# A two-sequence selective scan: the last 128 columns of the second sequence are given to GpSimd, and nobody scales u ahead any more

## The reference

```python
def step(h, inp):
    dt, bt, ct, xt = inp
    h = jnp.exp(dt[:, :, None] * A) * h + (dt * xt)[:, :, None] * bt[:, None, :]
    y = jnp.einsum('bdn,bn->bd', h, ct)
    return (h, y)
...
x = _layernorm(x + out_proj(y + x * D_param))
x = _layernorm(x + down(silu(gate(x)) * up(x)))
```

## Time and profile before

| | |
|---|---|
| median of 3 runs | 2693.13 us (2690.42 to 2694.03) |
| time of the profiled execution | 2687.74 us |
| its span, from first to last instruction | 2685.9 us |
| mean granted TensorE clock | 0.956 of full speed |
| instructions | 48350 |

### The profile page before, as it was taken

The page is one execution under the profiler, slowest core; times in us unless marked ns, Lnnn a source line. Parts: engine busy times, 40 slices in busy tenths (PEclk is TensorE's granted clock), DMA queues, the critical chain, the costliest instruction groups (busy, mean ns, idle before and its releaser), DMA issues.

```text
span 2685.9 us, 48350 instructions
## 1 busy us (share of the span) xinstructions
PE 2316.6 (86%) x17036; PEld 1290.5 (48%) x17036; DVE 2584.4 (96%) x4160; ACT 1708.6 (64%) x2229; POOL 1028.3 (38%) x1031
## 2 busy tenths in 40 slices
PE   7866678998789987899779997799977998899998
PEld 4322224554345543555345553455534554465567
DVE  6999999999999999999999999999999999999892
ACT  5687766667566665667656666566666667654643
POOL 2343333443434434344333443344333443344320
PEclk8999999999999989999889998899989999999899
DMA  4566665777667876678757786577866777788694
GB/s 171 197 213 227 228 236 211 281 277 270 237 223 277 284 266 223 238 275 292 254 195 247 279 290 243 201 267 277 278 241 209 279 279 271 239 289 308 228 357 151
DMA packets 192060, 672.16 MB, mean 250 GB/s; under 512 B 20944, under 2 KB 26064, under 8 KB 191824
## 3 DMA queue, kind: packets, MB, share of 16 engines
q1 hardware_dynamic: 152432, 544.02, 57.5%
q10 hardware_dynamic: 39392, 125.06, 13.3%
HBM read 660.61 MB, written 8.39 MB: 249 GB/s over the span
## 4 chain that ended last, share of the span: by engine, by line
PE 39%; DVE 28%; ACT 15%; issue 12%; DMA 6%; POOL 0%; ACTq 0%; DVEq 0%; POOLq 0%
DVE h L709 14%; PE banks L1200 11%; DVE banks L686 10%; PE banks L1036 10%; PE banks L1176 7%; PE banks L1276 7%; ACT a L981 6%; DVE h L706 4%; DMA u_bc<-u_scratch 4%; ACT L720 2%; DMA U<-in_xT 1%; PE banks L1128 1%; PE banks L1124 1%; ACT u_bc L1000 1%; ACT v L862 1%
## 5 line engine op out<-in xcount | busy, mean ns | idle before, releaser
L981 ACT ACTIVATE a<-banks 128x2048 f32<-128x2048 f32 x512 | 960.7, 1876 | 604.3 <-PE banks L1200 563.1
L686 DVE TENSOR_TENSOR banks<-a,h 128x512 f32<-128x512 f32 x2048 | 1324.1, 688 | 4.1 <-ACT a L981 4.1
L709 DVE SCALAR_TENSOR_TENSOR h<-u_bc,BCt,banks 128x512 f32<-128x512 f32 x1482 | 1038.2, 732 | 5.4 <-PE banks L1276 5.4
L581 POOL TENSOR_TENSOR dexp<-spread,dt 128x512 f32<-128x512 f32 x512 | 539.1, 1053 | 821.2 <-DVE banks L686 779.2
L1200 PE MATMUL banks<-dexp,A 32*128 32x256 f32 x8192 | 623.6, 421 | 150.6 <-ACT a L981 149.0
L1276 PE MATMUL banks<-h,cz 128*32 128x512 f32 x4096 | 667.9, 623 | 94.4 <-DVE h L706 64.7
L1200 PEld LDWEIGHTS banks<-dexp,A 32*128 32x128 f32 x8192 | 390.3, 195 | 484.4 <-ACT a L981 347.7
L1036 PE MATMUL banks<-vT,w_ring 128*128 128x256 f32 x1792 | 449.9, 394 | 7.6 <-ACT up L948 6.9
L1036 PEld LDWEIGHTS banks<-vT,w_ring 128*128 128x128 f32 x1792 | 323.8, 190 | 175.4 <-issue 118.2
L706 DVE TENSOR_TENSOR h<-u_bc,banks 128x512 f32<-128x512 f32 x566 | 367.5, 673 | 19.9 <-PE banks L1276 19.9
L593 POOL TENSOR_SCALAR u_bc<-u_bc,BCt 128x512 f32<-128x512 f32 x266 | 184.1, 692 | 404.6 <-DVE banks L686 394.3
(11 more groups left out here) (177 smaller groups left out, 1284.9 us busy)
## 6 DMA issues: line engine op xcount, KB each, us to landing
u_bc<-u_scratch SPq DMA_DIRECT2D x1021, 512.0 KB, 4.6
w_ring<-in_gu_w ACTq DMA_DIRECT2D x112, 512.0 KB, 5.5
w_ring<-in_down_w ACTq DMA_DIRECT2D x56, 512.0 KB, 5.7
a<-in_gu_w ACTq DMA_DIRECT2D x16, 512.0 KB, 12.7
a<-in_down_w ACTq DMA_DIRECT2D x8, 512.0 KB, 4.4
x_tok<-in_x_rows SPq DMA_DIRECT2D x15, 256.0 KB, 5.7
out_rows<-v ACTq DMA_DIRECT2D x15, 256.0 KB, 3.4
U<-in_xT ACTq DMA_DIRECT2D x7, 512.0 KB, 6.0
```

Source lines behind the costliest of these rows:

```text
L581: e.tensor_tensor(dexp[:, q % E_RING, :, :, :], spread[:, :].unsqueeze(1).unsqueeze(1).to_broadcast(shape), by_step[:, :, first:first + BS ...
L686: e.tensor_tensor(m_ps[:, b, :], a[:, blk % A_RING, b, s, :], h[:, (t - 1) % H_RING, b * D:(b + 1) * D], ALU.mult).then_inc(s_m, 1)
L709: e.scalar_tensor_tensor(h[:, t % H_RING, part], u_bc[:, t % U_RING, part], BCt[c % 2][:, 0, b * TB + tl:b * TB + tl + 1], m_ps[:, b, :], ...
L981: e.activation(dst.rearrange("p b t (x j) -> p x (b t) j", j=GP), src.rearrange("p g (i r j) -> p (g i) r j", i=PAIR, j=GP), ACT.Exp, scal ...
```

## The change

VectorE keeps the first sequence and columns 0 to 383 of the second, so its second product and its second sum are 384 columns wide. The last 128 columns (`SHARE`) are made by GpSimd alone, with three instructions a step in the new `share`: the product of `a` and h(t-1) into `m_share` in SBUF, u by B in place, and their sum into h(t). The sum waits for both by semaphore, and the next step's product for the sum (`s_hg`). All scaling of u ahead, by GpSimd and by ScalarE, goes, and with it line 706; VectorE always uses the scaling form. GpSimd no longer waits on `s_m` ahead of its diagonals and pieces. What reads h or frees u, `a` or B now also waits for GpSimd's semaphores. A matrix of one value becomes a broadcast column, which makes room for `m_share`.

```diff
-        even = range(FIRST_Z, SEQ - 4, 2)
-        on_pool = {(t + 2, 0): i for i, t in enumerate(
-            t for t in even if not any(stage in PIECES for stage, _ in at_steps(t, 2)))}
-        on_act = {place: i for i, place in enumerate(
-            place for t in even if quiet(t) and light(t) and light(t - 2) for place in ((t + 2, 1), (t + 3, 0), (t + 3, 1)))}
...
                 if t >= U_RING:
                     e.wait_ge(s_h, BATCH * (t - U_RING + 1))
+                    e.wait_ge(s_hg, t - U_RING + 1)
...
-            def scale(t):
...
+            def share(t):
+                c, blk, s, tl, slot = t // TB, t // BS, t % BS, t % TB, t % U_RING
+                part, of_b = slice(BATCH * D - SHARE, BATCH * D), slice(D - SHARE, D)
+                if s == 0:
+                    e.wait_ge(s_exp, 2 * (blk + 1))
+                if t:
+                    e.wait_ge(s_hg, t)
+                e.tensor_tensor(m_share[:, :], a[:, blk % A_RING, 1, s, of_b], h[:, (t - 1) % H_RING, part], ALU.mult
+                                ).then_inc(s_mg, 1)
...
+                e.tensor_scalar(u_bc[:, slot, part], u_bc[:, slot, part], BCt[c % 2][:, 0, TB + tl:TB + tl + 1], 1.0, ALU.mult,
+                                ALU.mult).then_inc(s_zg, 1)
+                if t >= H_RING:
+                    e.wait_ge(s_y, t - H_RING + 1)
+                e.wait_ge(s_mg, t + 1)
+                e.wait_ge(s_zg, t + 1)
+                e.tensor_tensor(h[:, t % H_RING, part], m_share[:, :], u_bc[:, slot, part], ALU.add).then_inc(s_hg, 1)
 
             for q in range(DEXP_AHEAD):
                 diagonals(q)
+            e.wait_ge(s_zero, 2)
             for t in range(SEQ):
                 c = t // TB
+                share(t)
                 if t in DEXP_AT:
-                    e.wait_ge(s_m, BATCH * (t + 1))
                     diagonals(DEXP_AT[t])
                 if t % 2:
                     for slot in range(SLOTS * (t % TB - 1), SLOTS * (t % TB + 1)):
                         for stage, x, j in plans[c].get(slot, ()):
-                            if stage in PIECES:
-                                e.wait_ge(s_m, BATCH * (t + 1))
                             piece_before(e, x, stage, j)
                             piece_behind(e, x, stage, j)
-                    if (t + 1, 0) in on_pool:
-                        e.wait_ge(s_m, BATCH * (t + 1))
-                        scale(t + 1)
...
+                return D - SHARE if b else D
...
-                    e.tensor_tensor(m_ps[:, b, :], a[:, blk % A_RING, b, s, :],
-                                    h[:, (t - 1) % H_RING, b * D:(b + 1) * D], ALU.mult).then_inc(s_m, 1)
+                    e.tensor_tensor(m_ps[:, b, 0:cols], a[:, blk % A_RING, b, s, 0:cols],
+                                    h[:, (t - 1) % H_RING, b * D:b * D + cols], ALU.mult).then_inc(s_m, 1)
...
                 e.wait_ge(s_h, BATCH * (t + 1))
+                e.wait_ge(s_hg, t + 1)
```

More of the change, by code:

```diff
@@ L29 @@
 U_RING = 5
+SHARE = 128
 E_RING = 4
@@ L62 @@
 DEXP_AT = {dexp_step(q): q for q in range(DEXP_AHEAD, TILES_P)}
-FIRST_Z = 24
 FIRST_U = 3
@@ L226, in build @@
         h = sb("h", [P, H_RING, BATCH * D])
+        m_share = sb("m_share", [P, SHARE])
         cz = sb("cz", [P, GP * (CZ_RING * BATCH * CS + 1)])
@@ L584, in diagonals @@
                                 ).then_inc(s_dexp, 1)
[L586 to L593 removed]
+            def share(t):
[7 more added lines that the diff above has]
+                                ).then_inc(s_mg, 1)
+                if t < FIRST_U:
+                    e.wait_ge(s_ucp, BATCH * (t + 1))
+                else:
+                    e.wait_ge(d_u[slot], 16 * (t // U_RING + (slot >= FIRST_U)))
+                if t == 0:
+                    e.wait_ge(s_bc, 1)
+                elif tl == 0:
+                    e.wait_ge(s_work, emptied("xp", c, 0))
+                e.tensor_scalar(u_bc[:, slot, part], u_bc[:, slot, part], BCt[c % 2][:, 0, TB + tl:TB + tl + 1], 1.0, ALU.mult,
[5 more added lines that the diff above has]
+                e.tensor_tensor(h[:, t % H_RING, part], m_share[:, :], u_bc[:, slot, part], ALU.add).then_inc(s_hg, 1)
             for q in range(DEXP_AHEAD):
                 diagonals(q)
+            e.wait_ge(s_zero, 2)
             for t in range(SEQ):
                 c = t // TB
+                share(t)
                 if t in DEXP_AT:
[L600 removed]
                     diagonals(DEXP_AT[t])
@@ L678, in vector, with width @@
             e.wait_ge(s_utc, BATCH)
+            def width(b):
+                return D - SHARE if b else D
             for t in range(SEQ):
@@ L758, in before @@
                         if x >= 2:
-                            e.wait_ge(*((s_cz, TB // CS * (x - 1)) if j else (s_h, BATCH * TB * (x - 1))))
+                            if j:
+                                e.wait_ge(s_cz, TB // CS * (x - 1))
+                            else:
+                                e.wait_ge(s_h, BATCH * TB * (x - 1))
+                                e.wait_ge(s_zg, TB * (x - 1))
                         dst = BCt[x % 2][:, j, :]
@@ L992, in window @@
                 last.then_inc(s_ycp, 1)
-            def scale(t, b):
-                c, tl, slot = t // TB, t % TB, t % U_RING
-                if tl < 4 and c:
-                    e.wait_ge(s_work, emptied("xp", c, 0))
-                e.wait_ge(d_u[slot], 16 * (t // U_RING + (slot >= FIRST_U)))
-                part = u_bc[:, slot, b * D:(b + 1) * D]
-                e.activation(part, part, ACT.Copy, scale=BCt[c % 2][:, 0, b * TB + tl:b * TB + tl + 1]).then_inc(s_za, 1)
             first_chunk()
@@ L1016, in scalar @@
                         exponents(EXP_AT[SLOTS * t + i], p_ps)
-                    if i == t % 2:
-                        for place in ((t + 2, 0), (t + 2, 1)):
-                            if place in on_act:
-                                scale(*place)
                     for stage, x, j in plans[c].get(SLOTS * (t % TB) + i, ()):
@@ L1055, in before @@
                     e.wait_ge(s_sq, x + 1)
-                    product(dst[:, 0:TC], [(mean_mat[:, :], T[:, k, :]) for k in range(KB)]).then_inc(s_ms, 1)
+                    product(dst[:, 0:TC], [(mean_col[:, :].to_broadcast([P, P]), T[:, k, :]) for k in range(KB)]).then_inc(s_ms, 1)
                 elif stage == "sel":
@@ L1213, in first_chunk @@
                 e.wait_ge(s_sqv, 1)
-                product(ms_first, [(mean_mat[:, :], T[:, k, :]) for k in range(KB)]).then_inc(s_ms, 1)
+                product(ms_first, [(mean_col[:, :].to_broadcast([P, P]), T[:, k, :]) for k in range(KB)]).then_inc(s_ms, 1)
                 e.wait_ge(d_wsel, 16)
```

28 lines of the change are left out of this document (10 added, 18 removed).

## The result

The changed kernel takes 3176.5 us in the median (3174.4 to 3179.1, 4 runs) against 2691.8 for the kernel before, a ratio of 1.181 (95% interval 1.178 to 1.184). The forecast of 3000 us had the sign, the mechanism and the range (2770 to 3290); 308 us more than before were forecast and 485 measured. The 60% case of the forecast, 2830 to 3170, was missed by 6 us; the measured time lies between it and the rival of both products in one piece.

A forecast was written before the change was run, and what follows sets the result against it. VectorE was taken to bound the kernel at 2.52 us a step; with GpSimd's share both engines were to run at 2.81: 48.7 + 1024 x 2.81 + 65.4 = 2991.5 us of span, rounded to 3000 us, range 2770 to 3290.

The forecast's parts named there:

- the rival of both products in one piece: GpSimd waits for VectorE's pair of products each time, 1.05 us a step: period 3.08 us, 3275 us; chance 16%.
- The bound now and the lock: VectorE sets the time, 2.52 us a step; GpSimd reading SBUF and VectorE instructions with two SBUF inputs don't run together.
- VectorE alone, 2.25 us a step: VectorE's steady period with 128 columns fewer in a product and a sum: 2.52 - 0.27 = 2.25 us.
- TensorE has room at the new period: TensorE's busy time of 2.23 us a step fits within the expected period of 2.81 us.
- GpSimd alone, 2.03 us a step: GpSimd's product, scaling, sum, diagonals, pieces and gaps: 0.41 + 0.40 + 0.45 + 0.49 + 0.28 = 2.03 us a step.
- The toll on GpSimd, 0.77: GpSimd meets each VectorE product once a step, losing 0.45 and 0.32 us: 2.03 + 0.77 = 2.80 us.
- The toll on VectorE, 0.59: VectorE's second product loses 0.34 us to a waiting GpSimd instruction, its first 0.25 to a remainder: 2.84 us a step.
- its two counts: The period counted on GpSimd, 2.80 us, and on VectorE, 2.84 us, taken to agree; 2.81 was used.
- Start and end: GpSimd's scan begins after the eighth diagonal at 48.7 us; the 65.4 us at the end stay untouched.
- No lock for short instructions: Only long GpSimd instructions clash, or GpSimd settles beside the sums; VectorE's 2.25 us rules: 2415 us; chance 6%.
- The waits' absorption: VectorE products falling into GpSimd's two 0.11 us result waits a step cost it less: 2.59 us, 2773 us; chance 14%.
- The strict lock: No overlap at all of VectorE's products with GpSimd's instructions: 3.27 us a step, 3470 us; chance 4%.

The follow-up runs named there:

- the run without the lock: The changed kernel with VectorE's products reading m_ps in PSUM in place of a in SBUF from the second token on: 2623.6 us, 0.975 of the kernel before.

## Why the prediction was right, and where it fell short

*The bound now and the lock: right.* The runs with the products reading PSUM show that the time is the lock: 553 us come back in the changed kernel, 387 in the kernel before without its waits.

*VectorE alone, 2.25 us a step: right*, with products of 689 and 552 ns and sums of 735 and 602 where nothing meets them. The forecast that TensorE has room at the new period held too; the granted clock was 0.948. Only in the first stretch (50 to 370 us of the trace), where the forecast had leaned on the 0.96 of the kernel before, was it 0.87, with TensorE busy for 224 of the 320 us; VectorE was busy for 318 of them all the same.

*GpSimd alone, 2.03 us a step: too low by 0.21, and this is the term that failed.* Taking the toll found below from the period leaves 2.99 - 0.75 = 2.24. The timeline of the run without the lock shows the parts, from one step's product to the next one's:

```profile
302.47 0.46 POOL L573 TENSOR_TENSOR m_share<-a,h 128x128 f32<-128x128 f32 x1
302.91 0.37 POOL L583 TENSOR_SCALAR u_bc<-u_bc,BCt 128x128 f32<-128x128 f32 x1
303.46 0.46 POOL L589 TENSOR_TENSOR h<-m_share,u_bc 128x128 f32<-128x128 f32 x1 [0.17 <-POOL u_bc L583]
304.06 0.46 POOL L573 TENSOR_TENSOR m_share<-a,h 128x128 f32<-128x128 f32 x1
```

Product to scaling is 0.44 (0.41 forecast), scaling to sum 0.55 (0.40), sum to the next product 0.60 (0.57). With these the forecast's own sum gives 0.44 + 0.55 + 0.46 + 0.49 + 0.28 = 2.22 (0.46 is its 0.45 with the 0.60). The scaling takes 0.375, not the 0.29 read off a one-input instruction of another kind, and the wait for its result costs 0.17, not 0.11, the mean of two cases. These two make 0.15 us, some 150 of the 186 us by which the span was missed; they were small numbers taken from far rows and multiplied by 1024. That such a gap is paid in full was shown by placing the scaling one step ahead.

*The toll on GpSimd, 0.77: right.* By the listed durations it is (774 - 459) + (792 - 375) + (1074 - 1051) / 2 ns and about 0.01 for the pieces, 0.75. It doesn't come as forecast in each step: at 684 steps the products are met one by one, for 0.44 and 0.30, at 268 both in one piece, for 0.83. So the rival of both products in one piece holds at a quarter of the steps, at 0.83 and not its 1.05, and the two forms cost nearly the same. That they do is luck: the forecast had no reason for it.

*The toll on VectorE, 0.59: too low.* It is (1190 - 689) + (775 - 552) ns = 0.72, and both terms were off: the second product pays 0.22, not 0.34, and the first 0.50, not 0.25. The first product doesn't come at any moment. It comes mostly 0.2 to 0.5 us behind the start of a diagonal or a piece, the longest instructions that GpSimd has, and pays for what is left: 1.24 or 1.33 us, and 1.55, instead of 0.69. With 2.25 + 0.72 = 2.97 VectorE comes out at the same rate as GpSimd. The forecast took it for a support that its two counts agreed (2.80 and 2.84). It was none: each was short by a term of its own, by 0.21 and 0.13. The range held the time because it took in a rival 275 us above the forecast.

*Start and end: right*, 48.9 and 65 us.

*The rivals.* No lock for short instructions: out, and its price was wrong as well. Without the lock, or without the share, the time is 2624 and not 2415 us, because TensorE stops it; I had called TensorE's 2.23 us room at 2.81 and not asked what it does at 2.25. The waits' absorption: out, for the gap between scaling and sum, by the scaling one step ahead. The strict lock: out, the handovers overlap as in the earlier trace rows: the product issued at 1501.72 had 0.98 us of the diagonal ahead of it and lost 0.84.

## What to carry to other kernels

An engine with 62% of its time idle may be idle so as not to be in the way: before giving it work, look at what its waits keep apart, and count GpSimd's reading and the bottleneck's instructions with two SBUF inputs as users of one resource. Much of the price of a chain that is walked a thousand times is in its gaps (here 203 us by one of them): take the wait for a result from a row, and look which instruction can be moved into it. And ask of every offload what the next engine does at the new period: here three quarters of the gain (270 us less 66) would have gone, most of it in waits for TensorE.

## What the runs showed of the hardware that was not expected

Two engines under the lock fell into a few fixed forms, though VectorE waits for no semaphore of GpSimd: of 1024 scalings 695 are listed with some 0.67 us, 268 with 1.20 and 61 with the 0.37 that they take alone. Under the lock an instruction is listed as busy while it waits, so the page's shares of 97% and 90% are waits in good part: of the 2855 us of GpSimd 2078 remain in the run without it, and of the 3080 of VectorE 2344. And a one-input instruction of 128 columns on GpSimd took 375 ns as scaling and 292 when it builds the identity, a difference as large as that between the scaling and the two-input product (459): the kind of instruction counts as much as its inputs.
